# A fused spectral and deformable convolution: one step as TensorE's loop body, with single buffers

## Chip, cores and metric

One Trainium2 chip, one of its cores. The metric is the device time of one execution in microseconds (us).

## What is computed

The input is x, (8, 32, 128, 128) in fp32. Two residual layers follow one another; `_gn` normalises each channel of each image on its own.

```python
def reference(x, ...):
    x = x + _L0_conv_ref(_gn(x), ...)   # means over rows and columns, 16 DFT modes each way, and a 1x1 mix
    x = x + _L1_conv_ref(_gn(x), ...)   # modulated deformable 3x3 convolution
    return x

def _L1_conv_ref(x, w_om, b_om, weight, bias):
    om = conv3x3(x, w_om) + b_om                # 27 channels: 9 dy, 9 dx, 9 masks
    mask = jax.nn.sigmoid(om[:, 18:])
    ys, xs = dy + ky + base_y, dx + kx + base_x
    vals = bilinear_sample(x, ys, xs) * mask    # 9 taps for each output pixel
    return einsum('bckhw,ock->bohw', vals, weight) + bias
```

## The kernel before, in words

The eight images are two groups (`g`) of four; a group's four images with 32 channels each fill the 128 partitions. The first layer and the statistics take the first tenth of the time: loads, row and column sums, a small DFT, the mix as matmuls (loop of lines 965 to 968). It leaves the sum x1 and its normalised copy with a padded border (xh) in DRAM.

The rest is the second layer, and all of the change lies there. It goes over 130 sets: a set is a pair of image rows for one group, with one extra set per group (`NSET` = 65, `SETS` = 130). For each set and each tile of 2 x 4 output pixels a matrix (the "table", `A`) says with which weight each of the 60 pixels of a 6 x 10 input region goes into each of 9 taps x 8 pixels; offsets of at most 2 pixels are covered, larger ones are found through `reach` and sent to a fallback that isn't entered here. The stages of a set are, with their line in the kernel before:

- `load_rows` (L393 to 402, SP): three DMAs bring the rows for the offset convolution into `wino`, which has two halves. `load_window` (L384) brings the six rows of the sampling region into `win`.
- `offsets` (L1018, matmuls L1025, PE): the 3x3 convolution for offsets and masks into `pM`; ACT copies it to `om_s` (L618); `turn_offsets` (L1029, L1035) turns it so that pixels lie on partitions.
- ACT takes the sigmoid (L636), DVE subtracts the five shifts (L802), ACT takes Abs (L609) and Relu (L627), which gives the hat functions `HT`; GpSimd multiplies masks in (L524) and makes the 5 x 5 products `prod` (L484), DVE turns them in blocks of 32 x 32 into `PT` (`turn`, L756).
- `spread` (L971, L982, PE): three rounds per set put them into the form of the table in the four banks of `pE`; ACT and DVE copy half of each round into `A` (L603, L774), which has two copies.
- GpSimd cuts the tiles' regions from `win` into `strips` (L514), PE transposes them (`turn_rows`, L1007, L1013: four parts of four tiles), ACT copies them into `XT` (L596).
- `gather` (L986, L1002, PE): for each tile and image a matmul of the region with the table, in three groups of 5, 5 and 6 tiles (`VGROUPS`), into `pV`; ACT and DVE copy the samples into `VS` (L590, L790), which has two copies.
- `convolve` (L1039, L1050, PE): nine taps as matmuls in four 64 x 64 tiles of the array, with the samples of two neighbouring sets, since the pixels of a tap row are kept so that half of them belong to the set before (`PRE`, `PLACES`). DVE adds bias and x1 (L783) and SP stores the result (L428).

Each engine has a written-out order of these stages, its `step(N, ...)`. In PE's step N (L1053) stand spread 0 of set N, convolve of set N - 3, gather 0 of set N - 1, and so on, offsets of set N + 3 in the middle. SP's step N (L408) is: `load_rows(N + 4)`, which waits until the offsets of set N + 2 are done (`om_done`), `load_window(N + 1)`, the load of x1's rows for set N - 2, and the store of set N - 3, which waits for `out_ready`. Every queue is worked off in order; semaphores tie them.

`steps` (L278) writes steps -3 to 4 out, puts 56 steps of a group in a loop, writes the 9 between the groups out, loops over 56 again and writes the rest out. The loop's body is two steps for PE, DVE and SP (`UNROLL` = 2) and four for ACT and GpSimd (`RING` = 4), since buffers are chosen by the step's parity.

Of the kernel before, what the change touches and what calls it, by code (L numbers as in the profile page):

```python
# [10 lines left out]
ALU = mybir.AluOpType  # L11
# [4 lines left out]
C = 32  # L16
# [35 lines left out]
VGROUPS = [(0, 5), (5, 10), (10, 16)]  # L52
NG = len(VGROUPS)
PRE = ROWS // 2

# [12 lines left out]
UNROLL = 2  # L68


def build(nc, g_count, x, wxr, wxi, wyr, wyi, mixt, mixb, womt, bom, wct, biasc,
          dft, inv, ident_d, perm, sel, cols, gtab, out):
    ctx = ExitStack()
    with ctx:
# [19 lines left out]
        sizes = [AW, AW, VW, VW, NTP * P, NTP * P, 2 * RPX, UW, RING * UW, 2 * OMW, 2 * NTP * P]  # L94
# [3 lines left out]
        A, VS, XT = areas[0:2], areas[2:4], areas[4:6]  # L98
        PT = areas[6].rearrange("p (s n) -> p s n", s=2)
        U = areas[7]  # L100
        HT = areas[8].rearrange("p (f s n) -> p f s n", f=2 * KS, s=RING)

        wino = areas[9].rearrange("p (s b r x) -> p s b r x", s=2, b=IPG, r=TILE_R)
        strips = areas[10].rearrange("p (s t h x) -> p s t h x", s=2, t=NTP, h=2)
# [28 lines left out]
        outs = sb("outs", [P, 2, TILE_R, W])  # L133
        om_s = sb("om_s", [P, PX])
        msk = sb("msk", [P, 2, KS * PB])
        reach = sb("reach", [P, 2 * KS * PB])
        prod = sb("prod", [P, 2, PB, BLK])
# [43 lines left out]
        pV = [pb(f"pV{i}", [P, 512]) for i in range(2)]  # L181
        pMR = pb("pMR", [P, 2 * 512])
        pM, pR = pMR[:, 0:512], pMR[:, 512:1024]
        pO = pMR[:, :].rearrange("p (r n) -> p r n", r=2)[:, :, PX:PX + W]
# [33 lines left out]
        wino_ld = [sem(f"wino_ld{i}") for i in range(2)]  # L218
# [22 lines left out]
        conv_done = sem("conv_done")  # L241
        out_ready = sem("out_ready")
# [29 lines left out]
        def outs_before(c, g, q=None):  # L272

            if q is None:
                return c - g
            return (c - q) - (2 * g if q == 0 else 0)

        def steps(eng, step, unroll):  # L278

            def stages(N):
                live = [0 <= N + k < SETS for k in (0, -1, -3, 3, 2, 1, -2)]
                live[2] = live[2] and (N - 3) % NSET < NPAIR
                live[6] = live[6] and (N - 2) % NSET < NPAIR
                return live

            def peeled(first, end):
                for N in range(first, end):
                    step(N, N % RING, stages(N), lambda n: divmod(n, NSET))  # L290
            peeled(-3, 5)
            for g in range(g_count):
                first, loops = g * NSET + 5, (NSET - 6) // RING * (RING // unroll)
                with eng.Fori(0, loops) as j:
                    for u in range(unroll):
                        step(j * unroll + (first + u), (first + u) % RING, [True] * 7,
                             lambda n, g=g: (g, n - g * NSET))
                peeled(first + loops * unroll, (g + 1) * NSET + 5 if g + 1 < g_count else SETS + 2)

        def convolved(c, place):  # L300

            if isinstance(c, int):
                return len([k for k in range(c + 1) if k % NSET < NPAIR])
            return outs_before(c, place(c)[0]) + 1

        def evacuate(q, gi, h):

            t0, t1 = VGROUPS[gi]
            dst = VS[q].rearrange("p (n x) -> p n x", x=W)[:, :, (h * NTP + t0) * TILE_C:(h * NTP + t1) * TILE_C]
            return dst, pV[h][:, 0:(t1 - t0) * TAPC].rearrange("p (n x) -> p n x", n=ROWS * KS)  # L310

        def expanded(q, r, h):

            src = pE[:, h * 1024:(h + 1) * 1024].rearrange("p (a n) -> p a n", a=2)[:, :, 0:EPX]
            dst = A[q].rearrange("p (n r a m) -> p r a n m", n=SLOT, r=ROUNDS, a=QUADS)
            return dst[:, r, 2 * h:2 * h + 2], src.rearrange("p a (m n) -> p a n m", n=SLOT)

        def tiles_of(q, h):

            w = win[:, q, 0:WIN_R, LEFT - KS + h * NTP * TILE_C:LEFT - KS + h * NTP * TILE_C + WIN_C]  # L320
            return bass.AP(w.tensor, w.offset, [w.ap[0], [TILE_C, NTP], [PADC, WIN_R], [1, WIN_C]])

        def rounds(on, N, r, ahead):

            k, rn = divmod(r + ahead, ROUNDS)
            return (N + k, k, rn) if on[(0, 5)[k]] else None
# [4 lines left out]
        def _(sp):  # L331
# [52 lines left out]
            def load_window(n, q, place):  # L384

                g, local = place(n)
                wait(sp, strips_done, n - 1)
# [5 lines left out]
            def load_rows(n, q, place):  # L393

                g, local = place(n)
                src = local * (TILE_R * PADC)
                wait(sp, om_done, n - 1)
                sp.nop(nofuse=True)
                for ky in range(KS):
                    rows = xh_d[g * P:(g + 1) * P, bass.ds(src + (TOP - 1 + ky) * PADC, TILE_R * PADC)]  # L400
                    sp.dma_start(wino[ky * C:(ky + 1) * C, q, :, :, :].rearrange("c b r x -> c b (r x)"),
                                 rows.rearrange("(b c) n -> c b n", b=IPG)).then_inc(wino_ld[q], 16)

            def halves_of(t, g, local, h):

                return t[g * P:(g + 1) * P, bass.ds(local * PX + h * W, W)].rearrange("(r p) n -> p r n", r=2)

            def step(N, s, on, place):  # L408
                q = s % 2
                if isinstance(N, int) and N == -3:  # L410
                    load_rows(0, 0, place)
                if not isinstance(N, int) or N + 4 < SETS:
                    load_rows(N + 4, q, place)
                if on[5]:
                    load_window(N + 1, 1 - q, place)
                if on[6]:
                    g, local = place(N - 2)
                    wait(sp, out_ready, outs_before(N - 2, g) - 1)
                    sp.nop(nofuse=True)
                    for h in range(TILE_R):  # L420
                        sp.dma_start(x1r[h * HALF:(h + 1) * HALF, q, :, :], halves_of(x1_d, g, local, h)) \
                            .then_inc(x1_ld[q], 16)
                if on[2]:
                    g, local = place(N - 3)
                    sp.wait_ge(out_ready, outs_before(N - 3, g) + 1)
                    sp.nop(nofuse=True)
                    for h in range(TILE_R):
                        sp.dma_start(halves_of(out, g, local, h), outs[h * HALF:(h + 1) * HALF, 1 - q, :, :]) \  # L428
                            .then_inc(out_st[1 - q], 16)
            steps(sp, step, UNROLL)  # L430
# [39 lines left out]
        def _(pool):  # L470
# [7 lines left out]
            def product(n, kx, buf, first, end, at):  # L478

                m = end - first  # L480
                hy = ring[:, kx, first * NSH:end * NSH].rearrange("p (m s o) -> p m s o", s=NSH, o=1)
                hx = ring[:, KS + kx, first * NSH:end * NSH].rearrange("p (m o s) -> p m o s", s=NSH, o=1)
                shape = [P, m, NSH, NSH]
                return nc.gpsimd.tensor_tensor(  # L484
                    prod[:, buf, at:at + m, 0:SQ].rearrange("p m (a b) -> p m a b", a=NSH),
                    hy.to_broadcast(shape), hx.to_broadcast(shape), ALU.mult)
# [696 lines left out]
```

## Time and profile before

| | us |
|---|---|
| median of 2 runs | 2603.17 (2598.89 to 2607.45) |
| the profiled execution | 2619.18 |
| its span | 2617.3 |
| busy: PE matmul, PE weight load | 1998.2, 1456.0 |
| busy: DVE, ACT, GpSimd | 1332.1, 1088.3, 851.8 |

The span runs from the first to the last instruction of the profiled execution; what lies around it makes up its own time. Busy times overlap. The granted TensorE clock was 0.892 of full speed on the mean.

### The profile page before, as it was taken

The page shows a single profiled execution, that of the slowest core. Times are in us where ns is not written, and L with a number is a line of the kernel's source. Part 1 is how long each engine was busy: PE and PEld are TensorE (multiplying, and loading weights), DVE is VectorE, ACT ScalarE, POOL GpSimd, SP SyncE. Part 2 cuts the span into 40 slices and gives each one's busy share as a digit, 9 for nine tenths or more (in the row PEclk, how much of TensorE's full clock was granted, in tenths as well). Part 3 has the DMA queues.
Part 4 walks back from the last instruction along what each step waited for, and adds up shares of the span by engine and source line. Part 5 has one row for each costly group of instructions (what it writes and reads, how often), then busy time and mean ns, then how long its engine had stood idle before and what let it go on. Part 6 is the DMA issues. An engine that isn't in the chain of part 4 may idle for free.

```text
span 2617.3 us, 141297 instructions
## 1 busy us (share of the span) xinstructions
PE 1998.2 (76%) x61533; PEld 1456.0 (56%) x61533; DVE 1332.1 (51%) x2068; ACT 1088.3 (42%) x1858; POOL 851.8 (33%) x893
## 2 busy tenths in 40 slices
PE   8553587777878778777788887778777878778786
PEld 3310366665656566665566665556555655556565
DVE  8696354444444454444455554444444444454444
ACT  0013454444434444444445544444444434344443
POOL 0000343333333333333334433333333333333331
PEclk9698698888888888898999998899989989899899
DMA  7046422222222222222222222222222222222221
GB/s 283 17 179 271 136 74 67 66 61 70 63 62 65 61 71 58 67 71 57 69 71 72 69 72 67 57 71 63 64 56 69 70 55 71 54 71 62 64 58 27
DMA packets 162224, 204.86 MB, mean 78 GB/s; under 512 B 20288, under 2 KB 136672, under 8 KB 157536
## 3 DMA queue, kind: packets, MB, share of 16 engines
q1 hardware_dynamic: 161632, 195.34, 25.3%
q8 instruction: 571, 9.36, 1.5%
q14 instruction: 21, 0.17, 0.0%
HBM read 143.05 MB, written 52.22 MB: 75 GB/s over the span
## 4 chain that ended last, share of the span: by engine, by line
PE 65%; issue 19%; DVE 8%; ACT 4%; DVEq 2%; DMA 1%; ACTq 0%; SPq 0%
PE pV L1002 17%; PE pMR L1050 15%; PE pE L982 11%; PE pMR L1013 9%; PE pMR L1025 7%; PE pMR L1035 4%; DVE big L737 2%; ACT big L596 2%; DVE big L760 2%; DVE big L802 1%; ACT big L609 1%; DMA xh_scratch<-win 1%; DVEq L737 1%; DVE stats L672 1%; PE pV L937 1%
## 5 line engine op out<-in xcount | busy, mean ns | idle before, releaser
L484 POOL TENSOR_TENSOR prod<-big 128x600 f32<-128x600 f32 (+1 forms) x489 | 503.2, 1038 | 1208.0 <-DVE big L760 1195.9
L982 PE MATMUL pE<-big,sel_s 32*64 32x192 f32 x12480 | 429.6, 365 | 319.3 <-issue 318.4
L1002 PE MATMUL pV<-big 60*32 60x72 f32 x33280 | 470.7, 232 | 89.4 <-issue 87.1
L790 DVE COPY big<-pV 128x360 f32<-128x360 f32 (+1 forms) x390 | 217.4, 557 | 627.8 <-PE pV L1002 627.8
L774 DVE COPY big<-pE 128x768 f32<-128x768 f32 x390 | 367.4, 942 | 292.6 <-PE pE L982 283.4
L603 ACT ACTIVATE big<-pE 128x768 f32<-128x768 f32 x390 | 331.9, 851 | 439.5 <-PE pE L982 439.5
L1002 PEld LDWEIGHTS pV<-big 60*32 60x32 f32 x33280 | 384.9, 106 | 207.7 <-issue 206.5
L590 ACT ACTIVATE big<-pV 128x360 f32<-128x360 f32 (+1 forms) x390 | 191.7, 492 | 709.2 <-PE pV L1002 708.9
L982 PEld LDWEIGHTS pE<-big,sel_s 32*64 32x64 f32 x12480 | 252.5, 142 | 405.6 <-issue 391.0
L1050 PE MATMUL pMR<-big,wc 64*64 64x128 f32 x9216 | 400.9, 338 | 43.3 <-DVE big L802 29.0
L1050 PEld LDWEIGHTS pMR<-big,wc 64*64 64x64 f32 x9216 | 356.2, 174 | 107.5 <-issue 107.1
L760 DVE STREAM_TRANSPOSE big<-prod 128x768 f32<-128x768 f32 x390 | 378.1, 970 | 0.0
L1013 PE MATMUL pMR<-ident,big 128*128 128x128 f32 x2080 | 339.4, 286 | 30.5 <-ACT big L596 29.6
L596 ACT ACTIVATE big<-pMR 128x512 f32<-128x512 f32 x520 | 307.7, 592 | 13.2 <-PE pMR L1013 1.2
L1013 PEld LDWEIGHTS pMR<-ident,big 128*128 128x128 f32 x2080 | 229.8, 146 | 105.8 <-ACT big L596 63.4
L514 POOL COPY big<-win 128x960 f32<-128x960 f32 x260 | 248.8, 986 | 0.6 <-DMA win<-xh_scratch 0.6
L1025 PE MATMUL pMR<-big,wom 96*32 96x256 f32 x3120 | 200.3, 389 | 47.4 <-DMA big<-xh_scratch 44.8
L783 DVE SCALAR_TENSOR_TENSOR outs<-pMR,bias_s,x1r 128x256 f32<-128x256 f32 x128 | 61.9, 484 | 266.7 <-PE pMR L1050 266.7
L524 POOL TENSOR_TENSOR big<-big,msk 128x360 f32<-128x360 f32 x130 | 107.1, 824 | 248.6 <-ACT big L627 248.6
L1025 PEld LDWEIGHTS pMR<-big,wom 96*32 96x32 f32 x3120 | 88.1, 110 | 118.1 <-issue 70.6
L802 DVE TENSOR_TENSOR big<-pMR,cols_s 128x720 f32<-128x720 f32 x130 | 116.6, 897 | 52.0 <-ACT msk L636 52.0
L1035 PEld LDWEIGHTS pMR<-perm_s,om_s 128*128 128x128 f32 x780 | 98.9, 194 | 40.1 <-issue 35.5
(70 smaller groups left out, 971.0 us busy)
## 6 DMA issues: line engine op xcount, KB each, us to landing
big<-xh_scratch SPq DMA_DIRECT2D x390, 136.0 KB, 2.6
win<-xh_scratch SPq DMA_DIRECT2D x130, 408.0 KB, 3.9
xh_scratch<-win SPq DMA_DIRECT2D x32, 544.0 KB, 2.7
big<-in_x SPq DMA_DIRECT2D x16, 1024.0 KB, 15.5
x_scratch<-big SPq DMA_DIRECT2D x16, 1024.0 KB, 3.9
x1r<-x_scratch SPq DMA_DIRECT2D x256, 64.0 KB, 3.2
out<-outs SPq DMA_DIRECT2D x256, 64.0 KB, 2.2
xh_scratch<-zero SPq DMA_DIRECT2D x4, 204.0 KB, 2.7
```

What stands on the lines that cost most here:

```text
L484: return nc.gpsimd.tensor_tensor(prod[:, buf, at:at + m, 0:SQ].rearrange("p m (a b) -> p m a b", a=NSH), hy.to_broadcast(shape), hx.to_bro ...
L514: last = nc.gpsimd.tensor_copy(strips[:, 1 - s % 2, :, h, 0:REG].rearrange("p t (r x) -> p t r x", r=WIN_R), tiles_of(1 - s % 2, h))
L596: nc.scalar.activation(XT[q][:, k * 512:(k + 1) * 512], pR[:, :], ACT.Copy).then_inc(xt_done, 1)
L603: nc.scalar.activation(*expanded(q, r, 0), ACT.Copy).then_inc(e_act, 1)
L760: nc.vector.transpose(PT[:, buf, :], prod[:, buf, :, :].rearrange("p m k -> p (m k)")) \
L774: nc.vector.tensor_copy(*expanded(q, r, 1)).then_inc(e_dve, 1)
L790: nc.vector.tensor_copy(*evacuate(1 - q, r, 1)).then_inc(v_dve, 1)
L982: last = mm(o[:, i2::TILE_R], sel_s[part, i2 * KS + rn, :], src[:, i2::TILE_R, :, h * NTP:(h + 1) * NTP], start=True, stop=True)
L1002: last = mm(o[:, :, x, :], XT[q][part, t * P + b * C:t * P + (b + 1) * C], A[q][part, at:at + TAPC], start=True, stop=True)
L1013: last = nc.tensor.transpose(pR[:, u * P:(u + 1) * P], strips[:, q, k * TPC + u, :, :].rearrange("p h x -> p (h x)"), ident[:, :])
L1025: last = mm(pM[b * C:(b + 1) * C, 0:PX], wom[:, kx, :], wino[0:KS * C, q, b, :, x0:x0 + W], start=(kx == 0), stop=(kx == KS - 1))
L1050: last = mm(pO[i * HALF:(i + 1) * HALF, r, :], wc[part, k, :], src[part, m, kx, :], start=(k == 0), stop=(k == TAPS - 1))
```

## The change

- PE's loop body becomes one step. For PE, ACT and GpSimd a single loop runs over sets 5 to 126; DVE and SP keep two loops with two steps in the body.
- `A`, `VS`, `XT`, `wino` and `strips` have one copy each in place of two; `PT` and `prod` have three (one for each kx).
- A round of `spread` is now two units (`ROUND_OF`): a unit is one kx for half of the tiles. Each of its matmuls has 96 columns where it had 192, and there are twice as many. ACT copies a round in two instructions, DVE in one (`both_units`). The first half of the tiles is complete after two of the three rounds.
- `gather` goes in four groups of four tiles; `pV` is also where `convolve` writes (`pO` is now a view of it), each after the copies of the samples.
- `convolve(n)` uses the samples of one set only. What belongs to the rows of this set goes to one part of the result and what belongs to the set before to the other; DVE keeps the first sum, with x1 added, in `begun`, and adds it a step later (two DVE instructions where there was one).
- `load_rows(N + 3)` moves from the head of SP's step to its end.

The core of the diff:

```diff
             def step(N, s, on, place):
                 q = s % 2
-                if isinstance(N, int) and N == -3:
-                    load_rows(0, 0, place)
-                if not isinstance(N, int) or N + 4 < SETS:
-                    load_rows(N + 4, q, place)
-                if on[5]:
+                if on[1]:
                     load_window(N + 1, 1 - q, place)
-                if on[6]:
-                    g, local = place(N - 2)
-                    wait(sp, out_ready, outs_before(N - 2, g) - 1)
+                g, local = place(N)
+                if on[0] and not (isinstance(local, int) and local == NPAIR):
+                    wait(sp, conv_read, N - 1)
...
-                if on[2]:
-                    g, local = place(N - 3)
-                    sp.wait_ge(out_ready, outs_before(N - 3, g) + 1)
+                g, local = place(N - 1)
+                if on[-1] and not (isinstance(local, int) and local == 0):
+                    sp.wait_ge(out_ready, N - 1 - g)
...
+                if on[3]:
+                    load_rows(N + 3, place)
-            steps(sp, step, UNROLL)
+            steps(sp, step, 2, True)

-            def load_rows(n, q, place):
+            def load_rows(n, place):
...
-                wait(sp, om_done, n - 1)
+                wait(sp, om_done, n)

+            def output(n, q, place):
...
+                dve.wait_ge(conv_done, n + 1)
+                if not first:
+                    wait(dve, out_st[q], of_parity(n, g, q, 0) * 16)
+                    nc.vector.scalar_tensor_tensor(out=outs[:, q, :, :], in0=pO[:, :, W:2 * W],
+                                                   scalar=bias_s[:, 0:1], in1=begun[:, 1 - q, :, :],
+                                                   op0=ALU.add, op1=ALU.add).then_inc(out_ready, 1)
+                if not last:
+                    dve.wait_ge(x1_ld[q], of_parity(n, g, q, NPAIR) * 16 + 32)
+                    nc.vector.tensor_tensor(begun[:, q, :, :], pO[:, :, 0:W], x1r[:, q, :, :], ALU.add) \
+                        .then_inc(conv_read, 1)

+            def step(N, s, on, place):
+                if on[-1]:
+                    samples(N - 1, 2)
+                if on[2]:
...
+                    nc.vector.tensor_tensor(U.rearrange("p (m k) -> p m k", k=NSH), off.to_broadcast(shape),
+                                            grid.to_broadcast(shape), ALU.subtract).then_inc(sub_done, 1)
+                if on[0]:
+                    turn(N, 2)
+                    table(N, 0)
+                if on[-1]:
+                    samples(N - 1, 3)
+                if on[0]:
+                    table(N, 1)
+                if on[-1]:
+                    output(N - 1, 1 - s % 2, place)
+                if on[1]:
+                    turn(N + 1, 0)
...
+                if on[0]:
+                    samples(N, 0)
+                    table(N, 2)
+                if on[1]:
+                    turn(N + 1, 1)
+                if on[0]:
+                    samples(N, 1)
+            steps(dve, step, 2, True)

+            def spread(n, j):
+                pe.wait_ge(pt_done, n * KS + (2, 3, 3)[j])
+                wait(pe, e_act, n * ROUNDS + j)
+                wait(pe, e_dve, n * ROUNDS + j)
+                for c, (half, kx) in enumerate(ROUND_OF[j]):
+                    for i2 in range(TILE_R):
+                        for h, u in itertools.product(range(2), range(QUADS)):
...
+                            last = mm(o[:, i2::TILE_R], sel_s[part, i2 * KS + kx, :],
+                                      src[:, i2::TILE_R, :, t0:t0 + HTP], start=True, stop=True)

             def step(N, s, on, place):
+                if on[-1]:
+                    gather(N - 1, 2)
                 if on[0]:
-                    spread(N, 0, q)
...
+                    spread(N, 0)
+                    turn_rows(N, 2)
+                if on[-1]:
+                    gather(N - 1, 3)
+                if on[0]:
+                    turn_rows(N, 3)
+                    spread(N, 1)
+                if on[-1]:
+                    convolve(N - 1)
+                if on[3]:
+                    offsets(N + 3)
+                if on[0]:
+                    gather(N, 0)
+                    spread(N, 2)
                 if on[1]:
+                    turn_rows(N + 1, 0)
                 if on[0]:
+                    gather(N, 1)
                 if on[1]:
+                    turn_rows(N + 1, 1)
                 if on[3]:
                     turn_offsets(N + 3)
-            steps(pe, step, UNROLL)
+            steps(pe, step, 1)
```

The parts of the diff are, in this order: SP's step, `load_rows`, DVE's output and step, PE's spread and step. ACT's step is now: samples 2 of set N - 1, table 0 and rows 2 of set N, samples 3 of N - 1, Abs of N + 2, rows 3 and table 1 of N, Relu of N + 2, `om_s` of N + 3, samples 0 and table 2 of N, rows 0 of N + 1, samples 1 of N, rows 1 of N + 1, masks of N + 3.

`offsets(n)` waits for `wino_ld` of 48 (n + 1): for all three DMAs of `load_rows(n)`.

## Rows read from the trace of the kernel before

**Rows 1.** The page: its head, and the chain that ended last, by engine.
```profile
span 2617.3 us, 141297 instructions
...
PE 65%; issue 19%; DVE 8%; ACT 4%; DVEq 2%; DMA 1%; ACTq 0%; SPq 0%
```
**Rows 2.** Timeline of PE (start, length, instructions, idle before), 1500 to 1550 us.
```profile
1520.19 1.50 PE L1025 MATMUL pMR<-big,wom 96*32 96x256 f32 x24
1521.62 1.08 PE L1002 MATMUL pV<-big 60*32 60x72 f32 x80
1522.63 0.66 PE L1013 MATMUL pMR<-ident,big 128*128 128x128 f32 x4
1523.21 0.91 PE L982 MATMUL pE<-big,sel_s 32*64 32x192 f32 x32
1524.05 0.86 PE L1035 MATMUL pMR<-perm_s,om_s 128*128 128x108 f32 x6
...
1528.86 2.28 PE L1050 MATMUL pMR<-big,wc 64*64 64x128 f32 x72 [0.97 <-DVE big L802]
...
1542.25 0.34 PE L1002 MATMUL pV<-big 60*32 60x72 f32 x11 [0.70 <-issue]
1546.06 1.59 PE L982 MATMUL pE<-big,sel_s 32*64 32x192 f32 x32 [3.47 <-issue]
```
**Rows 3.** Windows: us, busy time by engine (instructions), clock granted, DMA share, GB/s.
```profile
1372.40:1506.00 133.60, 113.66 (x4037) 84.82 (x4021) 74.89 (x104) 69.21 (x121) 56.44 (x58) 0.97 0.26 71
...
1506.00:2536.20 1030.20, 797.43 (x26462) 594.99 (x26460) 487.33 (x676) 452.43 (x790) 366.26 (x380) 0.91 0.24 64
...
1546.00:1552.00 6.00, 5.77 (x104) 4.57 (x104) 0.96 (x1) 0.85 (x1) 0.37 (x1) 0.51 0.02 5
```
**Rows 4.** The page: the instruction queue (packets, MB, share of 16 engines).
```profile
q8 instruction: 571, 9.36, 1.5%
```
**Rows 5.** DMA queues in the stretch of one loop turn, 1800.2 to 1834.7 us.
```profile
q8 instruction: 9, 0.15, 1.8%
```
**Rows 6.** DMA queues, 120 to 235 us: all that moved anything.
```profile
q1 hardware_dynamic: 4444, 24.61, 52.1%
q14 instruction: 1, 0.01, 0.0%
```
**Rows 7.** Groups by line and form, 1000 to 1400 us: busy, mean ns, idle before.
```profile
L760 DVE STREAM_TRANSPOSE big<-prod 128x768 f32<-128x768 f32 x68 | 66.0, 970 | 0.0
L774 DVE COPY big<-pE 128x768 f32<-128x768 f32 x68 | 64.3, 945 | 55.6 <-PE pE L982 53.9
...
L603 ACT ACTIVATE big<-pE 128x768 f32<-128x768 f32 x68 | 57.9, 851 | 91.0 <-PE pE L982 91.0
L596 ACT ACTIVATE big<-pMR 128x512 f32<-128x512 f32 x90 | 53.4, 593 | 2.0
...
L802 DVE TENSOR_TENSOR big<-pMR,cols_s 128x720 f32<-128x720 f32 x22 | 19.7, 897 | 0.0
```
**Rows 8.** Timeline of all engines, 1515 to 1517 us: convolution's end and output.
```profile
1514.79 0.40 PE L1050 MATMUL pMR<-big,wc 64*64 64x128 f32 x8
...
1515.43 0.48 DVE L783 SCALAR_TENSOR_TENSOR outs<-pMR,bias_s,x1r 128x256 f32<-128x256 f32 x1 [2.52 <-PE pMR L1050]
```
**Rows 9.** Timeline of SP, 1500 to 1537 us: length is that of issue.
```profile
1516.15 1.50 SPq L428 DMA_DIRECT2D out<-outs  x2
...
1521.96 1.34 SPq L401 DMA_DIRECT2D big<-xh_scratch  x3
1523.63 0.36 SPq L389 DMA_DIRECT2D win<-xh_scratch  x1
```
**Rows 10.** Timeline, 274 to 300 us: the first load of rows and who waits.
```profile
277.07 14.22 SPq L401 DMA_DIRECT2D big<-xh_scratch  x12
...
280.82 2.79 PE L1025 MATMUL pMR<-big,wom 96*32 96x256 f32 x24 [44.80 <-DMA big<-xh_scratch]
```
**Rows 11.** The view of line L401: from issue to landing of one load.
```profile
DMA to landing us min/median/max: 2.2/2.6/4.3
```

More of the change, by code:

```diff
@@ L270, in wait, with of_parity @@
                 eng.wait_ge(s, v)
[L272 to L286, printed above, removed]
+        def of_parity(n, g, q, skipped):
+            return (n - q) - 2 * sum(1 for k in range(2) if (k * NSET + skipped) % 2 == q and
+                                     (k < g or (k == g and skipped == 0)))
@@ L288, in peeled, with steps, looped @@
+        def steps(eng, step, unroll, apart=False):
             def peeled(first, end):
                 for N in range(first, end):
[L290 to L293, printed above, removed]
+                    step(N, N % RING, {k: 0 <= N + k < SETS for k in range(-1, 4)}, lambda n: divmod(n, NSET))
+            def looped(first, end, g):
+                loops = (end - first) // unroll
@@ L294, in steps @@
                 with eng.Fori(0, loops) as j:
                     for u in range(unroll):
[L296 removed]
+                        step(j * unroll + (first + u), (first + u) % RING, {k: True for k in range(-1, 4)},
                              lambda n, g=g: (g, n - g * NSET))
[L298 to L304, printed above, removed]
@@ L318, in tiles_of @@
[L318 to L326, printed above, removed]
+                return first + loops * unroll
+            at = -3
+            for g in range(g_count if apart else 1):
+                peeled(at, g * NSET + 5)
+                at = looped(g * NSET + 5, ((g + 1) * NSET if apart else SETS) - 3, g)
@@ new lines, in cut_tiles @@
+            def cut_tiles(n, q, half):
+                if half == 0:
+                    pool.wait_ge(win_ld[q], (n - q) * 8 + 16)
+                wait(pool, t_done, (n - 1) * TCH + 2 * half + 2)
+                pool.nop(nofuse=True)
+                for h in range(2):
+                    last = nc.gpsimd.tensor_copy(
+                        strips[:, half * HTP:(half + 1) * HTP, h, 0:REG].rearrange("p t (r x) -> p t r x", r=WIN_R),
+                        tiles_of(q, h, half))
+                last.then_inc(strips_done, 1)
@@ L804, in _, with samples, table, turn @@
-            steps(dve, step, UNROLL)
+            def samples(n, k):
+                dve.wait_ge(v_done, n * TCH + (k + 1))
+                nc.vector.tensor_copy(*evacuate(k, 1)).then_inc(v_dve, 1)
+            def table(n, j):
+                dve.wait_ge(e_done, n * ROUNDS + (j + 1))
+                nc.vector.tensor_copy(*both_units(j, 2)).then_inc(e_dve, 1)
+            def turn(n, kx):
+                dve.wait_ge(prod_done, n * KS + (kx + 1))
+                wait(dve, e_done, (n - 1) * ROUNDS + (2, 3, 3)[kx])
+                nc.vector.transpose(PT[:, kx, :], prod[:, kx, :, :].rearrange("p m k -> p (m k)")) \
+                    .then_inc(pt_done, 1)
@@ new lines, in output @@
+            def output(n, q, place):
+                g, local = place(n)
+                first = isinstance(local, int) and local == 0
+                last = isinstance(local, int) and local == NPAIR
+                dve.wait_ge(conv_done, n + 1)
[8 more added lines that the diff above has]
+                        .then_inc(conv_read, 1)
+                else:
+                    dve.wait_ge(out_ready, n - g)
+                    dve.sem_inc(conv_read, 1)
```

427 lines of the change are left out of this document (186 added, 241 removed).

## The prediction

> **What bounds the kernel now.** First the page's head and the chain that ended last [rows 1]: TensorE's matmuls are 65% of the chain, and 19% is "issue", time in which PE waits for nothing the profile shows; ACT and DVE together are 12%. So PE's own stream sets the end. Next the timeline of PE [rows 2], and in it the idle before each phase. At full clock a phase costs, start to start: four transposes 0.58 us, offsets 1.43, a gather of 80 records 1.01, a spread 0.84 (32 records of 192 columns), the turned offsets up to 0.86, the convolution 2.28. A step (4 + 1 + 3 + 3 + 1 + 1 of them) is 12.6 us. Waits for other engines are small: 0.97 before the convolution. But eleven records before the loop's end stands 0.70 us of "issue", and after its branch 3.47 more.
>
> The windows [rows 3] give the price. Nine steps written out (1372 to 1506) take 133.6 us, 14.8 each; 56 steps in the loop of two take 1030.2, 18.4 each, with the clock down from 0.97 to 0.91. By the code a step is 470 matmul records and as many weight loads (each fp32 matmul of lines 982, 1002, 1025, 1035 and 1050 is two, a transpose one). The instruction queue moved 571 packets, 9.36 MB, 16 KB each [rows 4]; at 64 bytes an instruction that is 146,000, against 141,297 executed. So PE's two-step body (some 1,930 instructions, 7.6 packets) is fetched anew on every turn. One turn (1800.2 to 1834.7) has 9 of them [rows 5]. In 120 to 235 us, where PE's loop body is two matmuls (lines 965 to 968), no packet of that queue is there at all [rows 6]: a short body stays.
>
> **The change, part by part.** *PE's stream.* Convolution (72 records), offsets (24), transposes (16) and turned offsets (6) keep number and shape. Gathers: 256 records in four groups of 64 instead of 80, 80, 96. A group costs between 64/80 of 1.01 = 0.81 and 1.01; I take 0.88, four = 3.5 (was 3.35 in the rows' way of counting). Spreads: 64 records of 96 columns each in place of 32 of 192. If columns decide, 0.84; if records decide, 1.68; the gather's 12.6 ns a record shows that far more records than 26 ns each pass, so I take 0.90, three = 2.7. Sum of a step: 2.3 + 1.4 + 3.5 + 2.7 + 0.8 + 2.3 = 13.0 us (12.7 to 15.5).
>
> *The body.* 940 + 192 = 1,132 matmul and load instructions a step and some 40 waits: 1,170, 4.6 packets, so 5 or 6 blocks and the one fetched ahead: at most 7. The body of before touches 9 and misses on all, as it must in any store of fewer than 9. No row shows whether 7 stay: the bounds are a body of a few instructions, for which nothing is fetched, and one of 1,930. I take that they stay, since the short body shows a fetcher that looks for its target in what it holds, and put the other bound in as a rival. If they stay, all "issue" at fetches goes: of the 18.4 us a step some 3.5.
>
> The Trainium skill ("Runtime: NRT & Kernel Launch", Instruction fetch mechanics) states that PE's instruction memory is 128 KiB, 2,048 instructions, filled in 16 KiB blocks, and also that a taken branch out of the current two-page window forces a fetch. By the first sentence the new body stays, by the second it is fetched each step. The trace agrees with the block size and with the refetch of 9 blocks; it doesn't tell the two sentences apart.
>
> *Single buffers, ACT and DVE.* A step's work: ACT copies 4 x 0.4 (samples of 288 elements, by the slope of its two copies), 6 x 0.46 (a table piece of 384 elements: 0.851 - 384 x (0.851 - 0.593)/256), 4 x 0.59 and the rest 2.4: 9.2 us; DVE 3 x 0.95, 3 x 0.97, 4 x 0.45, 0.90 and some 1.4: 9.9 [rows 7]. Neither is the bound, but each handover is now close. Walking one step: after gather 2 ends at 0, spread 0 ends at 0.9; DVE copies samples (to 0.5), subtracts (1.5), turns (2.5) and only then copies the table (3.5), which spread 1 needs; PE gets there at 3.2, so it waits 0.4. ACT copies two table pieces (0.95 to 1.9) before the rows (2.5), which transposes 3 want at 2.3: 0.3. One more of 0.25 at transposes 1. About 0.9 in all (0.3 to 2): a step of 13.9.
>
> *The load of the offsets' rows.* This decides. `wino` was double and loaded a set ahead, at the head of SP's step; now it is single, and `load_rows(N + 3)` stands last in SP's step N, behind the wait for `out_ready` of set N - 1 and the store. That output needs `convolve(N - 1)`, which stands in PE's step N just before `offsets(N + 3)`, and offsets waits for this very load. So in every step the chain lies bare between two neighbours on PE: convolution's end (1514.79 + 0.40) to DVE's output 0.24; the output 0.48 [rows 8]; semaphore and SP's registers to the first store 0.24; two stores issued 1.50; the next semaphore and registers 0.33, as between SP's loads for the offsets and its window load [rows 9]; and from the first of three loads to the matmul that waits for them 3.75, as the very first load shows: issued at 277.07, PE starts at 280.82 [rows 10]. Sum 6.5. The third load is issued about 1.0 after the first, and from issue to landing it is 2.2 to 4.3, median 2.6 [rows 11]: the sum is bounded by 6.0 and 8.1. Queued behind offsets on PE are gather 0 and everything after; DVE and ACT wait for those. Nothing hides it; DVE's turn and ACT's leftovers only fill 1 to 2 us of it. Before, such a wait stands at the first set alone.
>
> *The clock.* After the 3.47 us gap at the branch the granted clock is 0.51 in 1546 to 1552 (all but at 1.2 GHz) [rows 3]. A gap of 6.5 in each step will do at least that. At 1.2 GHz offsets take 2.79 against 1.50 [rows 2, 10]. About 5 us after each gap at the low level: offsets 1.3, gather 0 0.5, half of spread 2 0.4: 2.2 us a step (1 to 3.5).
>
> Step: 13.9 + 6.5 + 2.2 = 22.6 us. The store of set 65 does not exist, so one step is spared.
>
> *Ends.* The first three loads follow one another: each waits for the offsets before it, 3.7 + 2.8, so step 0 starts at about 302. Steps 0 and 1 have no store in SP's way: 15.5 each, 333. Steps 2 to 126: 125 x 22.6 = 2825, less 6.5 + 2.2 once. Steps 127 to 130 have no offsets; with the close 50. Together 3199 in the span, 3201 with what lies around it; the profiled execution of before is 2619.18 for a median of 2603.17 (0.994), so 3180.
>
> *Nothing for the rest.* The second output addition (0.48 on DVE) lies within the gap; the store's order against x1r costs issue time on SP alone; POOL has 6.7 us of work in a step.
>
> **Rivals.** *Not kept (13%).* The 7 blocks don't stay. Then each step has a branch gap (3.5 to 5 us; 3.47 in rows 2), and blocks full of gathers and spreads, used up in some 2 us each, against the 3.8 us between packets now (9 in 34.5): 3.8 more; clock 1.2; less the 0.7 of waits that they cover: 8 us. 333 + 125 x 30.6 + 60 gives 4218, runs 4190. For it: 9 blocks are refetched on each turn, and nothing shows a body of several blocks that stays. Against: bodies within a block or two stay, so the fetcher does look whether it has the target. The skill's sentence on the two-page window is this rival.
>
> *Load not in the way (3%).* The opposite side: rows reach `wino` before PE is at offsets, if SP's order were other than I read it. Then the step is 13.9 at full clock, 302 + 130 x 13.9 + 15 = 2124, runs 2110: faster by a fifth. It decides where wait and clock cost together are under 4.0 us a step (333 + 125 x 17.9 + 50 is the time of before), a wait of some 3 us; store issue and load alone are over 5. So I hold it small.
>
> *Partly hidden (2%).* Wait about 3 and cost as before: within 2%.
>
> *Middle (5%).* Body kept, but spreads go by records (+2.3) and handovers cost 2 in place of 0.9: 26 a step, 3610. Against it the gather's 12.6 ns.
>
> **The numbers.** Forecast 77%: 3180, its own range 2990 to 3460 (steps of 21.1 to 24.9). The rivals above it are left out but for the edge: the range given is 2970 to 3500. Slower by over 2% (about what a measurement of this kernel tells from no change) 95%, within 2% 2%, faster 3%.
>
> **What would show it.** Right: between convolution and offsets PE idle 6 to 7 us, ended by the DMA into big; its issue on SP straight behind the stores; two levels of the clock in each step, granted mean near 0.8; instruction packets near 200 instead of 571; no "issue" at the branch. Spread 64 records in under 1 us. Wrong: no wait before offsets (then all falls), or over 800 instruction packets (the rival), or PE's bare step far from 13.

## The result, and the profile after

| | before | after |
|---|---|---|
| median of 2 runs, us | 2603.17 | 3096.4 (3096.13 to 3096.67) |
| ratio, with its 95% interval | | 1.1915 (1.1839 to 1.1991) |
| span of the profiled execution, us | 2617.3 | 3094.0 |
| granted TensorE clock, mean | 0.892 | 0.818 |
| instruction packets in the span | 571 | 45 |

The change makes the kernel slower by 19% (the two medians above give a quotient of 1.189). The forecast was 3180, its range 2970 to 3500. Each ratio in the experiments below is against runs of the kernel before taken beside that experiment; their medians are 2605.86 (experiments 1 to 3), 2589.20 (4 to 7), 2601.91 (8 and 9, a single run) and 2598.43 (10).

The page of the kernel after, its head, the busy times, the clock by slices, the instruction queue, the chain, and the first of the costliest groups:

```profile
span 3094.0 us, 168988 instructions
...
PE 2119.9 (69%) x74157; PEld 1560.3 (50%) x74157; DVE 1374.1 (44%) x2326; ACT 1159.0 (37%) x2378; POOL 889.9 (29%) x1153
...
PEclk9796888887888878888888888887888888888888
...
q8 instruction: 45, 0.74, 0.1%
...
PE 55%; DMA 12%; SPq 10%; issue 9%; ACT 7%; DVE 5%; DVEq 1%; ACTq 0%
...
L1047 PE MATMUL pM<-big,wom 96*32 96x256 f32 x3120 | 358.8, 628 | 827.9 <-DMA big<-xh_scratch 827.9
```

Two things changed against [rows 1] and [rows 4]. The instruction queue is all but silent: the body stays where PE can repeat it. And the chain, which had 1% of DMA and nothing of SP's queue, now has 12% and 10% of them. The last line says where: PE stood 827.9 us before the offsets' matmuls, all of it ended by the load of their rows.

The timeline of PE over two steps (start, length, instructions, idle before):

```profile
1501.01 2.79 PE L1047 MATMUL pM<-big,wom 96*32 96x256 f32 x24 [6.26 <-DMA big<-xh_scratch]
1503.73 1.26 PE L1026 MATMUL pVV<-big 60*32 60x72 f32 x64
1504.92 1.45 PE L1005 MATMUL pE<-big,sel_s 32*64 32x96 f32 x64
...
1509.10 0.88 PE L1026 MATMUL pVV<-big 60*32 60x72 f32 x64
1509.92 1.05 PE L1005 MATMUL pE<-big,sel_s 32*64 32x96 f32 x64
...
1514.14 2.20 PE L1079 MATMUL pVV<-big,wc 64*64 64x128 f32 x72
1522.80 2.79 PE L1047 MATMUL pM<-big,wom 96*32 96x256 f32 x24 [6.47 <-DMA big<-xh_scratch]
...
1543.90 2.79 PE L1047 MATMUL pM<-big,wom 96*32 96x256 f32 x24 [6.30 <-DMA big<-xh_scratch]
```

Between convolution (L1079) and offsets (L1047) PE stands idle in every step. Just after it offsets, gather and spread run at 2.79, 1.26 and 1.45 us; a few us later the same gather and spread take 0.88 and 1.05. The windows show the clock that goes with it (columns as in [rows 3]; these are the stretch after the gap, the rest of the step, and the next gap; the column before the last two is the granted clock):

```profile
1501.00:1507.00 6.00, 5.99 (x168) 3.78 (x176) 0.97 (x2) 1.40 (x4) 0.00 (x0) 0.58 0.21 76
1507.00:1516.00 9.00, 8.70 (x406) 7.59 (x408) 6.00 (x9) 7.10 (x16) 4.66 (x6) 1.00 0.00 0
1516.40:1522.80 6.40, 0.00 (x0) 0.00 (x0) 1.99 (x4) 0.00 (x0) 1.71 (x2) 0.76 0.43 103
```

0.58 is near the lower level, 1.2 GHz; 1.00 is 2.4 GHz. What fills the gap is in the chain of waits, followed over the same stretch:

```profile
1516.40 0.49 DVE outs L780
1517.22 0.65 SPq L425
1518.06 0.65 SPq L425
1519.03 0.33 SPq L402
1519.54 0.32 SPq L402
1520.04 2.72 DMA big<-xh_scratch
1522.80 2.79 PE pM L1047 x24
```

DVE's output (L780), two stores issued (L425), the first two of the three loads issued (L402), the third load up to its landing, and only then offsets. The whole middle of the run is like this: in the window 400 to 1900 us

```profile
400.00:1900.00 1500.00, 1048.04 (x39544) 797.72 (x39542) 629.00 (x978) 599.84 (x1259) 475.47 (x611) 0.82 0.19 51
```

39,544 matmul records at 566 a step (24 + 64 x 7 + 72 + 16 + 6) are 69.9 steps, 21.5 us each. The rows shown agree: from one offsets to the next it is 21.8 and then 21.1 us.

### The profile page after: what moved, and what is told of

Same layout as the page of the kernel before. It is cut to its first block, busy times and chain, and to the rows that moved or that the text cites. A ratio compares the mean times of both kernels' runs of the same rounds, so it can differ in the third digit from the quotient of the medians.

```text
span 3094.0 us, 168988 instructions
## 1 busy us (share of the span) xinstructions
PE 2119.9 (69%) x74157; PEld 1560.3 (50%) x74157; DVE 1374.1 (44%) x2326; ACT 1159.0 (37%) x2378; POOL 889.9 (29%) x1153
## 4 chain that ended last, share of the span: by engine, by line
PE 55%; DMA 12%; SPq 10%; issue 9%; ACT 7%; DVE 5%; DVEq 1%; ACTq 0%
PE pE L1005 14%; PE pM L1047 12%; DMA big<-xh_scratch 11%; PE pVV L1026 10%; PE pVV L1079 9%; PE pR L1035 7%; SPq L425 6%; SPq L402 4%; ACT big L599 4%; ACT big L594 3%; PE pM L1057 2%; DVE outs L780 2%; DVE big L736 2%; DMA xh_scratch<-win 1%; DVEq L736 1%
## 5 line engine op out<-in xcount | busy, mean ns | idle before, releaser
L1047 PE MATMUL pM<-big,wom 96*32 96x256 f32 x3120 | 358.8, 628 | 827.9 <-DMA big<-xh_scratch 827.9
L502 POOL COPY big<-win 128x480 f32<-128x480 f32 x520 | 289.5, 587 | 1818.8 <-PE pR L1035 1799.2
L1047 PEld LDWEIGHTS pM<-big,wom 96*32 96x32 f32 x3120 | 128.5, 163 | 976.5 <-DMA big<-xh_scratch 790.6
L1026 PE MATMUL pVV<-big 60*32 60x72 f32 x33280 | 512.6, 253 | 14.3 <-issue 12.2
L1026 PEld LDWEIGHTS pVV<-big 60*32 60x32 f32 x33280 | 409.5, 117 | 176.1 <-issue 170.2
L1005 PE MATMUL pE<-big,sel_s 32*64 32x96 f32 x24960 | 448.7, 274 | 19.6 <-issue 9.8
L1035 PE MATMUL pR<-ident,big 128*128 128x128 f32 x2080 | 362.1, 299 | 19.9 <-ACT big L599 1.9
L599 ACT ACTIVATE big<-pR 128x512 f32<-128x512 f32 x520 | 310.3, 597 | 45.2 <-PE pR L1035 40.9
L1079 PE MATMUL pVV<-big,wc 64*64 64x128 f32 x9360 | 287.9, 273 | 3.7 <-issue 3.1
L593 ACT ACTIVATE big<-pE 128x384 f32<-128x384 f32 x390 | 199.1, 510 | 232.3 <-PE pE L1005 232.3
L1079 PEld LDWEIGHTS pVV<-big,wc 64*64 64x64 f32 x9360 | 255.8, 133 | 19.9 <-issue 4.7
L594 ACT ACTIVATE big<-pE 128x384 f32<-128x384 f32 x390 | 195.5, 501 | 0.0
L780 DVE SCALAR_TENSOR_TENSOR outs<-pVV,bias_s,begun 128x256 f32<-128x256 f32 x128 | 61.9, 484 | 165.5 <-PE pVV L1079 165.5
```

The lines of the kernel that those rows point to most:

```text
L502: last = nc.gpsimd.tensor_copy(strips[:, half * HTP:(half + 1) * HTP, h, 0:REG].rearrange("p t (r x) -> p t r x", r=WIN_R), tiles_of(q, h, ...
L594: nc.scalar.activation(*unit_of(j, 1, 0), ACT.Copy).then_inc(e_act, 1)
L599: nc.scalar.activation(XT[:, k * 512:(k + 1) * 512], pR[:, :], ACT.Copy).then_inc(xt_done, 1)
L1005: last = mm(o[:, i2::TILE_R], sel_s[part, i2 * KS + kx, :], src[:, i2::TILE_R, :, t0:t0 + HTP], start=True, stop=True)
L1026: last = mm(o[:, :, t * TILE_C:(t + 1) * TILE_C, :], XT[part, x:x + C], A[part, at, :], start=True, stop=True)
L1035: last = nc.tensor.transpose(pR[:, u * P:(u + 1) * P], strips[:, k * TPC + u, :, :].rearrange("p h x -> p (h x)"), ident[:, :])
```

## The experiments

The theory was: the load's new place costs the whole loss and more (wait and clock), and the short body gains, by sparing PE its code fetch. The rivals: that the loss lies in the thinner spreads and in the handovers of single buffers; and that the short body gains nothing much, since the fetch is mostly hidden.

**1. The load at the head of SP's step.** All else as after.

```diff
                 q = s % 2
+                if on[3]:
+                    load_rows(N + 3, place)
                 if on[1]:
                     load_window(N + 1, 1 - q, place)
...
-                if on[3]:
-                    load_rows(N + 3, place)
             steps(sp, step, 2, True)
```

> Only SP's order differs from the changed kernel: load_rows(N + 3) stands first in step N, ahead of the waits for the store. Theory (the load lies bare between convolution and offsets): the wait of 6.4 us before offsets goes, and with it the low clock; a step falls from 21.4 to 15.3 - 2.0 = 13.3 us and the time to some 302 + 130 x 13.3 + 15 = 2050 us. Rival (the single buffers tie the engines so closely that another handover takes the wait's place): 15 us a step or more, 2270 us or more.

Measured: 2064.22 us (2062.44 to 2064.8), 0.793 of before (0.7899 to 0.7961). PE's timeline:

```profile
1503.84 1.50 PE L1047 MATMUL pM<-big,wom 96*32 96x256 f32 x24
...
1513.93 1.04 PE L1005 MATMUL pE<-big,sel_s 32*64 32x96 f32 x64 [0.17 <-DVE big L763]
...
1517.02 1.50 PE L1047 MATMUL pM<-big,wom 96*32 96x256 f32 x24
```

The gap is gone, offsets run at 1.50, and one step takes 13.1 to 13.2 us. Over 400 to 1900 us the window reads

```profile
400.00:1900.00 1500.00, 1471.80 (x64533) 1193.36 (x64536) 1033.63 (x1595) 975.91 (x2052) 764.60 (x999) 1.00 0.31 83
```

with the clock at 1.00 and PE busy 98% of the time. So one statement's place is worth 1032 us (3096.40 less 2064.22), and everything else in the change, single buffers and spreads of 64 records among it, is together a gain of 539 on the 2603.17 of before. The first rival, a loss in spreads and handovers, is out.

**2. The load between the wait for the output and the stores.** This splits the gap: the wait stays, the stores' issue leaves it.

```diff
-                if on[-1] and not (isinstance(local, int) and local == 0):
+                stores = on[-1] and not (isinstance(local, int) and local == 0)
+                if stores:
                     sp.wait_ge(out_ready, N - 1 - g)
                     sp.nop(nofuse=True)
+                if on[3]:
+                    load_rows(N + 3, place)
+                if stores:
+                    sp.nop(nofuse=True)
                     for i in range(TILE_R):
```

> As the changed kernel, but the load stands between the wait for out_ready and the two stores. Theory: the chain loses the stores' issue (1.50 + some 0.2), 6.4 -> 4.8 us of idle, so 125 x 1.6 = 200 us less in all, 2900 us, a little less if the clock comes back sooner. Rival (the idle is the transfer of the rows held up behind the stores' data, not their issue): the part from the first load's issue to offsets falls below 3.7 as well, and the gain is over 300 us.

Measured: 2908.55 (2906.64 to 2913.43), 1.1174 of before (1.113 to 1.1218).

```profile
1507.02 2.79 PE L1050 MATMUL pM<-big,wom 96*32 96x256 f32 x24 [4.65 <-DMA big<-xh_scratch]
...
1527.47 1.93 PE L1050 MATMUL pM<-big,wom 96*32 96x256 f32 x16 [4.63 <-DMA big<-xh_scratch]
```

The wait is 4.65 where it was 6.3 to 6.5: the stores' issue (1.49 in the chain above, 1517.22 to 1518.71) has left the chain. The time fell by 188 us, 1.5 a step. The clock falls as before (offsets still 2.79), so a gap of 4.65 costs the clock as much as one of 6.3. The stores' issue is a fifth of the load's price (188 of 1032); the rest is the wait for the output, the load's own issue and transfer, and the clock, which no experiment parts from one another.

**3. Experiment 1 with PE's body of two steps.** This undoes the body alone.

```diff
-            steps(pe, step, 1)
+            steps(pe, step, 2)
```

> As e1_load_first, but PE's loop body is two steps (some 2,330 instructions, 10 blocks). Theory (a body that doesn't fit is fetched anew, one block ahead): over 600 packets in the instruction queue, 3.5 to 5 us of idle at each branch, waits at blocks between, half the speed after each: 4 to 5 us a step more than e1, about 2600 us. Rival (the length of the body doesn't matter once the order is right, the idle called issue had another source): within 2% of e1.

Measured: 2963.92 (2952.74 to 2973.3), 1.1401 of before (1.1347 to 1.1456), and 900 us above experiment 1. The page:

```profile
span 2950.7 us, 168622 instructions
...
q8 instruction: 649, 10.63, 1.5%
...
PE 65%; issue 25%; DVE 4%; ACT 3%; DVEq 1%; DMA 1%; POOL 0%; SPq 0%; ACTq 0%; POOLq 0%
```

and PE's timeline at a branch:

```profile
1494.73 0.66 PE L1057 MATMUL pM<-perm_s,om_s 128*128 128x108 f32 x5
1499.94 1.25 PE L1026 MATMUL pVV<-big 60*32 60x72 f32 x64 [4.55 <-issue]
1501.12 1.23 PE L1005 MATMUL pE<-big,sel_s 32*64 32x96 f32 x38
1502.91 0.93 PE L1005 MATMUL pE<-big,sel_s 32*64 32x96 f32 x26 [0.57 <-issue]
```

The body is some 2,330 instructions, fetched in 10 packets on each turn. Its step takes some 20.5 us (66,437 matmul records in 2400 us), against 13.1 to 13.2 for the same work in experiment 1. The direction was as expected, the size wasn't: the expectation had put idle at the branch and at blocks, and the lower clock after it, at 4 to 5 us a step. In 400 to 2800 us PE's waits for "issue" alone are 579 us, 4.9 a step, and the whole difference is 7.4 (900 us over the loop's 122 steps). With this, the second rival (fetch mostly hidden) is out as well: the short body is worth 900 us.

**4. Before, with the load last and nothing else.** `wino` single, `load_rows(N + 3)` at the end of SP's step, all other parts as before.

```diff
-                if isinstance(N, int) and N == -3:
-                    load_rows(0, 0, place)
-                if not isinstance(N, int) or N + 4 < SETS:
-                    load_rows(N + 4, q, place)
...
+                if on[3]:
+                    load_rows(N + 3, place)
             steps(sp, step, UNROLL)
```

> The kernel before with one part of the change alone: a single wino, and load_rows(N + 3) last in SP's step, behind the store of set N - 3. Theory: the chain from convolution's end to offsets is as long as in the changed kernel, 6.4 us, but gather 0, two transposes and spread 1 stand between on PE, 3.0 us; 3.4 us lie bare, with the clock some 4 us a step, 130 x 4 = 500 us: about 3100 us. Rival (the idle at code fetches of the kernel before covers the load): under 2700 us.

Measured: 3068.25 (3061.21 to 3082.1), 1.1869 of before (1.1832 to 1.1906).

```profile
1510.01 2.79 PE L1023 MATMUL pMR<-big,wom 96*32 96x256 f32 x24 [2.59 <-DMA big<-xh_scratch]
...
1522.81 1.53 PE L980 MATMUL pE<-big,sel_s 32*64 32x192 f32 x32 [3.89 <-issue]
...
1534.15 2.36 PE L1023 MATMUL pMR<-big,wom 96*32 96x256 f32 x20 [3.28 <-DMA big<-xh_scratch]
```

The load's place alone makes the old kernel 479 us slower than the runs beside it. It costs less than the 1032 in the new one, and most of the difference is seen here: the old PE step has a gather, transposes and a spread between convolution and offsets, so the wait is 2.6 to 3.3 and not 6.3. The rest, some 1 us a step, may be that the clock of before was already partly lost at the branch (0.89 to 0.91 in its loops, against 1.00 in experiment 1); this was not tested.

**5 and 6. Experiment 1 with 300 and with 750 empty instructions in PE's body.** They were to find the length at which the body no longer stays.

```diff
+                for _ in range(300):
+                    pe.nop(nofuse=True)
```

> As e1_load_first, with 300 empty instructions between convolution and offsets: PE's body has 1,467 instructions, it touches 6 or 7 blocks and one ahead. Theory (PE keeps 8 blocks of 256 instructions): it stays, under 80 packets in the instruction queue; the time grows by what the 300 take to issue. Rival (it keeps only what the changed body needed, 7 blocks, or fewer by chance of place): over 600 packets.

> As e1_load_first, with 750 empty instructions: 1,917 in the body, 8 or 9 blocks and one ahead. Theory (8 blocks kept): it doesn't stay, 8 or 9 packets a turn, about 1,000 in the queue. Rival (what is kept is larger than 8 blocks, and the kernel before lost its body by its length of 1,934 with the one ahead only just): under 100 packets.

Measured, a single time each: 2065.51 and 2064.03 us, both with 168,988 instructions and 45 instruction packets, as experiment 1. By these counts the empty instructions left nothing in the program, so neither run says anything on the length. A body has to be lengthened with real work, as in 8 and 9.

**7. Experiment 1 with DVE's subtraction and ACT's Abs one stage later.** This is to remove the wait of 0.17 before spread 1. DVE's side is shown; the lines added here are taken out below the subtraction, and ACT's Abs moves behind `table(N, 1)` in the same way.

```diff
                 if on[-1]:
                     samples(N - 1, 2)
+                if on[0]:
+                    turn(N, 2)
+                    table(N, 0)
+                if on[-1]:
+                    samples(N - 1, 3)
                 if on[2]:
                     dve.wait_ge(msk_done, N + 3)
```

> As e1_load_first, but DVE subtracts after the table of round 0 and the last samples, and ACT takes Abs after table 1. Theory (in e1 PE waits for DVE before spread 1, 0.2 us a step, and DVE is late by the subtraction): up to 125 x 0.2 = 25 us less, 2040 us. Rival (that wait is replaced by one for ACT's rows or Abs): no change, or slower.

Measured: 2045.99 (2044.77 to 2047.38), 0.7905 of before (0.7889 to 0.7921).

```profile
1504.86 1.50 PE L1047 MATMUL pM<-big,wom 96*32 96x256 f32 x24
...
1517.83 1.50 PE L1047 MATMUL pM<-big,wom 96*32 96x256 f32 x24
```

No wait is left in the rows of this step, it takes 12.97 us, and this is the fastest of all versions.

**8 and 9. A longer body that is still one step.** In experiment 1 the gathers' matmuls are made twice (8), or twice in gathers 0 and 2 and three times in 1 and 3 (9); they write the same values again. This gives PE bodies of some 1,679 and 1,935 instructions.

```diff
-                for t in range(TPC):
+                for _, t in itertools.product(range(2), range(TPC)):         # 8
...
-                for t in range(TPC):
+                for _, t in itertools.product(range(2 + k % 2), range(TPC)): # 9
```

> As e1_load_first, with the matmuls of every gather made twice (the same values written again), so that PE's body has 1,679 instructions, 7 or 8 blocks of 256 and one ahead. It costs 4 x 0.5 = 2.0 us a step if nothing else changes, 2320 us. Theory (the body stays while its blocks and the one ahead are no more than 8): under 80 packets in the instruction queue if its place in memory gives 7 + 1, else 8 or 9 a turn, 1,000 and over 2900 us. Rival (what stays is smaller, 7 blocks in all): fetched anew in any case.

> As e8, with gathers 1 and 3 made three times: 1,935 instructions in PE's body, as many as the two-step body before, 8 or 9 blocks and one ahead. Work alone gives e1 + 125 x 3.0 = 2440 us. Theory (length decides, not that the body had two steps): 9 packets a turn, some 1,100 in the queue, 3.5 to 5 us at each branch and more at blocks, over 3200 us. Rival (something else of the two-step body made it be fetched): under 80 packets and about 2440 us.

Measured: 2403.14 and 4878.29 us, a single time each. The pages, 8 first:

```profile
span 2401.0 us, 235548 instructions
...
q8 instruction: 63, 1.03, 0.2%
```

```profile
span 4876.1 us, 268828 instructions
...
q8 instruction: 1161, 19.02, 1.7%
...
PE 65%; issue 31%; DVE 2%; DVEq 1%; DMA 1%; ACT 0%; POOL 0%; SPq 0%; ACTq 0%; POOLq 0%
```

The first stays: the extra work costs what it takes (a gather of 128 records 1.54 us, one of 64 0.89, so 4 x 0.65 x 130 = 338 us over 2064; the expectation had 0.5 for the 0.65). In 450 to 2200 us, inside its loop, no packet of that queue is on record. The second doesn't: 256 instructions more a step make the kernel twice as slow. So what matters is the length of the body and not the number of steps in it. By these two single runs the limit lies between 1,679 and 1,935 instructions; whether the place of the body in memory shifts it was not tried.

PE's timeline over one turn of 9's body, some of its gaps (the same gather comes again at 2037.84, after 35.5 us):

```profile
2002.30 0.94 PE L1026 MATMUL pVV<-big 60*32 60x72 f32 x39 [3.34 <-issue]
2005.09 1.68 PE L1026 MATMUL pVV<-big 60*32 60x72 f32 x89 [1.85 <-issue]
...
2024.86 0.34 PE L1026 MATMUL pVV<-big 60*32 60x72 f32 x11 [1.91 <-issue]
...
2033.22 0.43 PE L1026 MATMUL pVV<-big 60*32 60x72 f32 x18 [2.49 <-issue]
```

The pauses stand throughout the body and not only at its branch. In 400 to 4800 us PE's waits for "issue" are 1387 us in 971 pieces, the longest 3.3, over some 124 turns; one at each branch could be no more than 409 of them. That 9 would be over 3200 was expected; nearly 4900 wasn't.

**10. Before, with PE's body of four steps.** If packets set the time, a longer body that isn't kept either should be faster, since a turn's two partial blocks are shared by four steps. If only the pause at the branch counts, it comes half as often, which the expectation prices at 98 us or less.

```diff
-            steps(pe, step, UNROLL)
+            steps(pe, step, RING)
```

> The kernel before with four steps in PE's loop body in place of two (3,870 instructions, 15 or 16 blocks and one ahead at the branch). Theory (the kernel before is bound by code fetch throughout, at 4.05 us a packet of 256 instructions whether a branch is near or not): 16 or 17 packets for four steps in place of 18, 4.1 to 4.25 a step in place of 4.5; 112 steps x 0.25 to 0.4 x 4.05 = 110 to 180 us less, about 2450 us. Rival (only the idle at the branch counts, 3.5 us for two steps, and it is had half as often): 28 x 3.5 = 98 us less or under, 2500 us or more.

Measured: 2458.85 (2451.29 to 2467.28), 0.9475 of before (0.9439 to 0.9511). Its page has 516 packets for 571:

```profile
q8 instruction: 516, 8.45, 1.4%
```

It is 140 us under the median of the runs beside it. By the law below, 55 packets fewer would be worth 55 x 4.05 = 223 us, so the sign follows from packets and under two thirds of the size. This run doesn't tell packets from branches. The rival had priced a branch at 3.5 us. In before, 27 pauses at branches in the first loop sum to 134.8 us, 5.0 each, and 27 in the second to 100.3, 3.7 each; in this run 27 in the one and the other loop together sum to 96.0. The 139 us by which these fell are as much as was gained, so the rival, with its price put right, fits this run at least as well. What speaks against it stands elsewhere: the pauses in the middle of the body in experiments 3 and 9, and that the two loops of before, with branches of 5.0 and 3.7 us, take nearly the same time (1013.8 and 1030.2 us).

**The account.** The change in three parts, each the difference of two medians (before at 2603.17; against the runs beside experiment 3 the first part is 358):

| from | to | us |
|---|---|---|
| before | the new step, body of two steps, load first (3) | +361 |
| body of two steps | body of one step (1) | -900 |
| load first | load last (after) | +1032 |
| | sum | +493 |

The first part goes with more code: 168,622 instructions for 141,297, and 78 more packets. The profiled spans differ by 333 us, 4.3 us a packet; by the difference of the medians it is 4.6.

## Why the prediction was right

| term, us | forecast | measured |
|---|---|---|
| PE's bare step | 13.0 | 12.97 (experiment 7) |
| handover waits | 0.9 | 0.1 to 0.2 (13.1 to 13.2 in experiment 1, less 12.97) |
| wait for the load | 6.5 | 6.2 |
| clock | 2.2 | 2.2 (21.5 - 13.1 - 6.2) |
| step | 22.6 | 21.5 |
| the rest of the span | 374 (333 + 50 - 6.5 - 2.2) | 407 (3094.0 - 125 x 21.5) |

The steps are too long by 1.1 us, 138 us in all, and the rest of the span is too short by 33, so the sum of 3199 stands against a span of 3094. The last factor, 0.994 for the median against the profiled execution, took 20 us off the forecast; in the kernel after the two are the same within 0.3 us, so this factor brought the forecast nearer by chance.

The wait is (827.9 - 44.7)/126: its view for after, with the longest of them, 44.7, at the first set as in [rows 10], reads

```profile
PE pM L1047 <- DMA big<-xh_scratch: 827.9, 127, 44.7
```

- *The load decides.* Right, in its place, its links and its size. The reading that carried it was that SP's queue is in order: a load behind a wait for the output of convolution, for a matmul that follows that convolution on PE. The landing (1520.04 + 2.72) is within the bounds of [rows 11].
- *The clock.* Right: offsets 1.3, gather 0.4, spread 0.4 slower in the first step shown; in the second the spread is back at 1.05, so the loss differs from step to step. The forecast had 1.3, 0.5 and 0.4. The 2.2 of the table is what the other terms leave.
- *The body stays.* Right, with 45 packets, and none in 450 to 2900 us; "near 200" was too many. No row of before showed that a body of this length stays, as the prediction says: it was a bet, and it held.
- *Gather and spread.* Gather of 64: 0.82 start to start where spread or transposes follow at once, 0.95 where they don't, for 0.88 forecast; spread of 64 records: 0.97 for 0.90. Their errors cancel. Records of 96 columns thus take less than twice a spread of 32 with 192 (0.84 in [rows 2]): neither columns nor records alone decide, and the value chosen near the columns' end was right. (The 3.35 for the three gathers of before doesn't come out of [rows 2]: 256 records at 1.01 for 80 are 3.2. Nothing rests on it.)
- *Handover waits.* Over-sized: of the waits of 0.4, 0.3 and 0.25 only the first is seen; it measures 0.17 in experiment 1. This is 0.7 of the 1.1 by which the step was too long.
- *The step that failed* is a reading of before on which the sum didn't rest: that of its 18.4 us a step "some 3.5" go to fetches. Experiments 3 and 1, with the same work a step and the body as the only difference, are 7.4 us a step apart. The sum didn't feel it, since the new step was built from PE's phases at full clock and not by taking a saving off 18.4. Taking it off would have given 18.4 - 3.5 = 14.9 before the load, for 13.1 measured.
- *The rivals.* "Load not in the way" was to give 2110; where the load is first it is 2064. "Not kept" did not come, and was somewhat overpriced by the law below: a body of 1,170 instructions is at most 6 packets, and with the load wait a packet took 2500/525 = 4.76 us in experiment 4, so an estimate is 28.6 a step for the 30.6 forecast. It was not run.

## What the runs showed that was not expected

**Fetched code sets the pace of PE.** Where the body isn't kept and no load is waited for, the time is the number of instruction packets (16 KB, 256 instructions at 64 bytes) by about 4.05 us. In before, for 358.6 to 1372.4 us (the first loop), 1372.4 to 1506 (written out) and 1506 to 2536.2 (the second loop), the instruction queue reads

```profile
q8 instruction: 251, 4.11, 1.8%
...
q8 instruction: 33, 0.54, 1.7%
...
q8 instruction: 251, 4.11, 1.7%
```

and in experiment 3 (400 to 2800 us) and 9 (400 to 4800 us)

```profile
q8 instruction: 586, 9.60, 1.7%
```

```profile
q8 instruction: 1114, 18.25, 1.8%
```

| stretch | us | packets | us a packet |
|---|---|---|---|
| before, first loop | 1013.8 | 251 | 4.04 |
| before, written out | 133.6 | 33 | 4.05 |
| before, second loop | 1030.2 | 251 | 4.10 |
| experiment 3 | 2400 | 586 | 4.10 |
| experiment 9 | 4400 | 1114 | 3.95 |
| experiment 10, 400 to 2400 us | 2000 | 477 | 4.19 |

The work in a block differs far more than that. In before a step's phases at full clock are 12.6 us (the prediction's sum) for some 965 instructions (half of its 1,930), 3.3 us for 256 of them; in experiment 9 they are 12.97 + 6 x 0.65 = 16.9 us for 1,935, 2.2 us for 256. Yet the stretches agree within 6%. This is what speaks for the law; experiment 9 is the strongest case, since its work is worth 16.9 of the 35.5 us of a turn. By it, over the whole second layer the kernel before went at the pace at which its code came, the written-out stretch of [rows 3] included, and not at that of its matmuls. For the written-out stretch this rests on the one figure of 4.05, where 3.3 us of work, pauses and waits for other engines could add up to nearly as much. The profile shows only part of this as "issue" (19% of the chain): after a pause the matmuls run at the lower clock, as after the 4.55 us above, and count as busy.

The Trainium skill ("Runtime: NRT & Kernel Launch", Instruction fetch mechanics) gives PE 128 KiB in blocks of 16 KiB, 2,048 instructions, and the bodies agree: 1,679 stay, 1,935 (which with its partial blocks touches 9) don't. It also says that crossing a block is mostly hidden, and that a taken branch out of a two-page window forces a fetch. These runs disagree with both. Where the body isn't kept, PE stands at blocks in its middle (above), and they come one in some 4 us. A branch back over some 1,170 or over 1,679 instructions fetches nothing: the instruction queue has no packet in 450 to 2900 us of after, nor in 450 to 2200 us of experiment 8.

What a packet's 4 us consists of was not taken apart, nor was the limit found more closely than between those two lengths.

## What to carry to other kernels

Count the instructions of PE's loop body (no run here looks at the other engines'). If it is short enough to stay (1,679 here), it runs at the matmuls' pace. If not, each 256 instructions took about 4 us here, and fewer packets a step help: by fewer instructions or, as in experiment 10, by more steps in a body. Before the order of a DMA queue is touched, follow each load backwards: behind which wait it is issued, what releases that wait, and whether that is the instruction just ahead of the load's own consumer. A gap on PE in each step is paid twice, once as the gap and once more in the clock after it (here 6.2 and 2.2 us).
